# A four-layer cross-attention kernel: forty-eight projections go from plain float32 to three reduced-precision passes, and five hand-sized pieces of work move between engines

## The reference, cut to what matters

```python
# L0: cross-attention on ctx, 16 heads of 16, then an MLP (256 -> 1024 -> 256)
q = layer_norm(x) @ q_w + q_b;  k = ctx @ k_w + k_b;  v = ctx @ v_w + v_b
x = x + attention(q, k, v) @ cproj_w + cproj_b;  x = x + mlp(layer_norm(x))
# L1: queries from x, keys and values from [ctx, x] (256 keys), 16 heads of 16, then an MLP
q = x @ q_w + q_b;  k, v = split(concat([ctx, x]) @ kv_w + kv_b)
# L2: twice a cross-attention on ctx with 16 heads of 128 and one extra key and value, then an MLP
# L3: self-attention on x (w_qkv, mask), cross-attention on ctx (w_q, w_kv, mask), then an MLP
q, k, v = split(layer_norm(x) @ w_qkv + b_qkv)        # L3s
q = layer_norm(x) @ w_q + b_q;  k, v = split(ctx @ w_kv + b_kv)   # L3c
```

## Time and profile before

| | us |
|---|---|
| median of 3 runs | 1060.3 |
| lowest and highest | 1059.1 and 1060.75 |
| the profiled execution | 1061.92 |
| its span, first to last instruction | 1060.7 |
| stage A, layer 2, stage C (from the chain of waits, about) | 0 to 300, 300 to 805, 805 to 1060.7 |

### The profile page before, as it was taken

The page is one execution under the profiler, slowest core; times in us unless marked ns, Lnnn a source line. Parts: engine busy times, 40 slices in busy tenths (PEclk is TensorE's granted clock), DMA queues, the critical chain, the costliest instruction groups (busy, mean ns, idle before and its releaser), DMA issues.

```text
span 1060.7 us, 20845 instructions
## 1 busy us (share of the span) xinstructions
PE 1032.2 (97%) x8080; PEld 917.0 (86%) x8080; DVE 714.9 (67%) x1086; ACT 596.2 (56%) x1311; POOL 601.7 (57%) x627
## 2 busy tenths in 40 slices
PE   8999999999999999999999999999998999989988
PEld 7787888878888999999988999999998888778877
DVE  6987888899366565565567655665654378988751
ACT  6988788878633333223344223333226499999963
POOL 6874557465654344343287333553525689999860
PEclk9999999999999999999999999999999999999999
DMA  9200001000112222211130101110100000000000
GB/s 339 98 2 1 2 1 41 2 1 2 51 60 80 80 81 66 74 40 62 41 102 12 50 21 40 41 40 22 30 1 1 1 1 1 2 1 2 11 11 21
DMA packets 33786, 40.71 MB, mean 38 GB/s; under 512 B 2111, under 2 KB 31257, under 8 KB 32025
## 3 DMA queue, kind: packets, MB, share of 16 engines
q1 hardware_dynamic: 33689, 39.38, 11.4%
HBM read 38.32 MB, written 1.05 MB: 37 GB/s over the span
## 4 chain that ended last, share of the span: by engine, by line
PE 74%; POOL 8%; DVE 8%; ACT 5%; issue 5%; POOLq 0%; DVEq 0%; ACTq 0%
PE psum L789 14%; PE psum L683 9%; PE psum L671 8%; PE psum L803 7%; PE psum L849 7%; PE psum L709 5%; PE psum L837 5%; PE psum L817 4%; PE psum L602 4%; PE psum L699 3%; PE psum L724 2%; POOL C tile L1565 2%; PE psum L826 2%; PE psum L656 2%; ACT C tile L1364 2%
## 5 line engine op out<-in xcount | busy, mean ns | idle before, releaser
L1658 POOL TENSOR_TENSOR B tile<-B tile,B rec 128x1024 f32<-128x1024 f32 x32 | 60.8, 1899 | 204.2 <-DVE B rec L1150 204.2
L1571 POOL TENSOR_TENSOR A tile<-A tile,outer rec 128x1024 f32<-128x1024 f32 x48 | 90.7, 1897 | 74.7 <-DVE outer rec L1039 74.7
L1426 ACT ACTIVATE B own<-B max 128x8 f32<-128x8 f32 x32 | 6.7, 209 | 163.9 <-DVE B tile L1137 163.9
L1364 ACT ACTIVATE A tile<-A tile,outer min 128x128 f32<-128x128 f32 (+1 forms) x256 | 92.3, 452 | 6.1 <-DVE outer min L1032 6.0
L1282 ACT ACTIVATE B kT<-psum,B bcol 128x1024 f32<-128x1024 f32 x32 | 35.7, 1117 | 91.6 <-PE psum L789 91.6
L1364 ACT ACTIVATE C tile<-C tile,outer min 128x128 f32<-128x128 f32 x256 | 78.0, 402 | 2.1 <-DVE outer min L1032 2.1
L1178 DVE TENSOR_TENSOR x_all<-x_all,psum 128x512 f32<-128x512 f32 x64 | 42.6, 685 | 54.3 <-PE psum L849 54.3
L803 PE MATMUL psum<-B v hi,B cT hi 128*128 128x256 f32 x256 | 74.1, 289 | 0.3 <-ACT B kT L1282 0.3
L803 PE MATMUL psum<-B v hi,B cT lo 128*128 128x256 f32 x256 | 72.4, 283 | 0.0
L803 PE MATMUL psum<-B v lo,B cT hi 128*128 128x256 f32 x256 | 72.4, 283 | 0.0
L930 DVE TENSOR_SCALAR B qT<-psum,B bcol 128x1024 f32<-128x1024 f32 x32 | 41.1, 1283 | 43.3 <-PE psum L789 43.3
(11 more groups left out here) (240 smaller groups left out, 3362.4 us busy)
## 6 DMA issues: line engine op xcount, KB each, us to landing
weights<-in_weights_c SPq DMA_DIRECT2D x6, 1024.0 KB, 6.6
raw<-in_wq SPq DMA_DIRECT2D x32, 128.0 KB, 2.6
raw<-in_wk SPq DMA_DIRECT2D x32, 128.0 KB, 3.0
raw<-in_wv SPq DMA_DIRECT2D x16, 256.0 KB, 2.8
raw<-in_wo SPq DMA_DIRECT2D x16, 256.0 KB, 2.8
weights<-in_weights_a SPq DMA_DIRECT2D x1, 3072.0 KB, 21.7
weights<-in_weights_a SPq DMA_DIRECT2D x1, 2048.0 KB, 11.2
wide<-in_bias_v SPq DMA_DIRECT2D x2, 1024.0 KB, 11.5
```

What stands on the lines that cost most here:

```text
L1364: i = act.activation(of_head, of_head, ACT.Exp, bias=part.min[:, u % 4, h:h + 1], scale=-1.0)
L1571: pool.tensor_tensor(tile(u, ly.nk), tile(u, ly.nk), part.rec[:, u % 4, 0:ly.per].unsqueeze(2).to_broadcast([P, ly.per, ly.nk]), ALU.mult) ...
L1658: pool.tensor_tensor(tv, tv, m.brec[:, h, :].unsqueeze(2).to_broadcast([P, B, S]), ALU.mult).then_inc(s["normalised"].sem, s["normalised"] ...
```

## The change

- **Three passes** (`by_parts`, and `values`): keys and values of L0; queries, keys and values of L1; queries, keys and values of L3s; keys and values of L3c. The queries of L0 and of L3c stay float32. Each call has twelve fp32r matmuls in place of four float32 ones.
- **Their operands.** `ctxT_all` is gone: ACT writes the hi part of the context from PSUM at the start, DVE the lo part, and layer 2 uses the same two. `ctx_parts` goes. The input of L1 is drained by ACT (hi) and DVE (lo). That of L3s goes like that of an MLP: DVE applies scale and offset, ACT rounds, POOL subtracts.
- **Splitting their weights** (`wcut`): L0's key weights on ACT and DVE at the head of the lists; L0's value weights and the three of L1 on POOL in stage A; those of L3s on POOL in turns 5, 6 and 7 of the second attention, the two of L3c in turns 5 and 6.
- **MLP weights:** M2's four quarters are split in turns 1 to 4, L3c's four also in turns 1 to 4, behind the division of the second head, instead of in stage C.
- **The means' shares:** in stage C the shift is one DVE operation for both sequences instead of two on POOL.
- **All eight lists are written anew**, with other banks for many steps.
- The two `Bacc` constructors get `dynamic_dma_scratch_size=1024`.

```diff
@@ tensor_program
+    def by_parts(event, signal, drain, weights, src, k):
+        claim(d.take(event, k), drain, event)
+        for n in range(2):
+            for c in range(C):
+                for wp, sp in PASSES:
+                    i = pe.matmul(bank(k)[:, n * T:(n + 1) * T], weights[wp][:, c, n * P:(n + 1) * P], src[sp][:, c, :],
+                                  start=(c, wp, sp) == (0, 0, 0), stop=c == C - 1 and wp == 1)
+        i.then_inc(s[signal].sem, s[signal].mark(event))
...
-            by_features((name, "k", k, src), "k_projected", "k_drained", layers[name].wk, layers[name].sources(m, k)[src], 0, z)
+            by_parts((name, "k", k, src), "k_projected", "k_drained", m.w_parts[name, "k"], layers[name].sources(m, k)[src], z)
...
-                    i = pe.matmul(bank(z)[:, b * D:(b + 1) * D], ly.sources(m, k)[src][:, c, b * P:(b + 1) * P], ly.wv[:, c, :], start=c == 0, stop=c == C - 1)
+                    for wp, sp in PASSES:
+                        i = pe.matmul(bank(z)[:, b * D:(b + 1) * D], src[sp][:, c, b * P:(b + 1) * P], m.w_parts[name, "v"][wp][:, c, :],
+                                      start=(c, wp, sp) == (0, 0, 0), stop=c == C - 1 and wp == 1)
@@ vector_program
+            elif what == "xn" and st == "C":
+                name, of, k = a
+                dve.wait_ge(s["rstd_made"].sem, s["rstd_made"].at((name, of, k)))
+                dve.scalar_tensor_tensor(out=part.nb[k][:, :], in0=part.mv[k][:, :, 0], scalar=-1.0, in1=part.rstd[k][:, :], op0=ALU.mult, op1=ALU.mult).then_inc(
+                    s["shift_made"].sem, s["shift_made"].mark((name, of, k)))
+            elif what == "ctx":
+                k = a[0]
+                dve.wait_ge(s["ctx_hi_made"].sem, s["ctx_hi_made"].at(("ctx", k)))
+                dve.tensor_tensor(m.cT(k)[1], bank(d.bank["ctx", k]).rearrange("p (c t) -> p c t", c=C), m.cT(k)[0], ALU.subtract).then_inc(
+                    s["ctx_lo_made"].sem, s["ctx_lo_made"].mark(("ctx", k)))
+            elif what == "wcut" and tuple(a) == ("L0", "k"):
...
-            elif what == "ctx_parts":
...
@@ gpsimd_program
+    def cut_weights(name, which):
+        (hi, lo), raw, event = m.w_parts[name, which], m.w_raw[name, which], (name, which)
...
+        pool.tensor_copy(hi, raw).then_inc(s["w_hi_made"].sem, s["w_hi_made"].mark(event))
+        pool.wait_ge(s["w_hi_made"].sem, s["w_hi_made"].at(event))
+        pool.tensor_tensor(lo, raw, hi, ALU.subtract).then_inc(s["w_lo_made"].sem, s["w_lo_made"].mark(event))
...
-        if j == 2 and 2 <= turn < 5:
-            cut_up("M2", turn - 2)
+        if j == 2 and 1 <= turn < 5:
+            cut_up("M2", turn - 1)
+        if j == 2 and turn >= 5:
+            cut_weights("L3s", "qkv"[turn - 5])
...
         if turn:
             divide(j, turn, 1)
-        if last and j == 2:
-            pool.wait_ge(s["bv_drained"].sem, s["bv_drained"].at((2, NP_ - 1, 3)))
-            cut_up("M2", 3)
+        if j == 2 and 1 <= turn < 5:
+            cut_up("L3c", turn - 1)
+        if j == 2 and 5 <= turn < 7:
+            cut_weights("L3c", "kv"[turn - 5])
@@ the head of ORDER_ONE["PE"]
-    ctx 0 4, k L0 0 0 3, turn_in L0 in 0 5, ctx 1 7, q L0 0 4, k L0 1 0 5, scores 0, ctx 2 7, ctx 3 4, turn_in L0 in 1 5, scores 1, v L0 1 0 5,
+    ctx 0 0, turn_in L0 in 0 5, ctx 1 0, q L0 0 3, k L0 0 0 2, ctx 2 7, k L0 1 0 4, scores 0, k L0 2 0 7, ctx 3 5, v L0 2 0 4, scores 1,
@@ the head of ORDER_ONE["DVE"]
-    stats L0 in 0, xn L0 in 0, stats L0 in 1, q L0 0 4, stats L0 in 2, scores 0, minima 0, scores 1, even 0 0, minima 1, even 0 1, q L0 1 0,
+    stats L0 in 0, xn L0 in 0, ctx 0 0, stats L0 in 1, wcut L0 k, q L0 0 3, ctx 1 0, stats L0 in 2, stats L0 in 3, ctx 2 7, scores 0, minima 0, ctx 3 5,
```

More of the change, by code:

```diff
@@ L445 @@
+    up L1 3 2 5, up L1 3 4 7, up L1 3 6 0, turn_in L1 out 1 4, xn L1 out 2, parts 1, turn_in L1 out 0 2, parts 0, turn_in L1 out 2 3, xn L1 out 3,
+    keys_of 1, turn_in L1 out 3 7, parts 2, parts 3
 """,
     "DVE": """
-    stats L0 in 0, xn L0 in 0, stats L0 in 1, q L0 0 4, stats L0 in 2, scores 0, minima 0, scores 1, even 0 0, minima 1, even 0 1, q L0 1 0,
-    stats L0 in 3, even 1 0, scores 2, even 1 1, minima 2, scores 3, weigh 0, even 2 0, minima 3, weigh 1, even 2 1, q L0 2 2, project 1 5, project 0 0,
@@ L461 @@
-    down L1 2 1 0, stats L1 out 2, ctx_parts 1, ctx_parts 0, parts 1, down L1 3 0 0, parts 0, down L1 3 1 3, stats L1 out 3, parts 3, parts 2,
-    values_of 0, values_of 1, values_of 2, queries_of 1
+    stats L0 in 0, xn L0 in 0, ctx 0 0, stats L0 in 1, wcut L0 k, q L0 0 3, ctx 1 0, stats L0 in 2, stats L0 in 3, ctx 2 7, scores 0, minima 0, ctx 3 5,
+    scores 1, even 0 0, minima 1, even 0 1, q L0 3 3, q L0 1 0, even 1 0, scores 2, minima 2, even 1 1, even 2 0, weigh 0, scores 3, even 2 1, minima 3,
@@ L513 @@
+    up L3c 3 2 3, up L3c 3 4 0, up L3c 3 6 7
 """,
     "DVE": """
[L515 to L517 removed]
@@ L526 @@
-    turn_in L3c mlp 3 0, down L3c 2 0 7, down L3c 3 0 3, down L3c 3 1 7, down L3c 2 1 2
+    output 0, stats M2 mlp 0, output 1, xn M2 mlp 0, stats M2 mlp 1, xn M2 mlp 1, turn_in M2 mlp 0 0, output 2, stats M2 mlp 2, xn M2 mlp 2, output 3,
+    turn_in M2 mlp 1 1, stats M2 mlp 3, turn_in M2 mlp 2 5, down M2 0 0 7, down M2 0 1 3, stats L3s in 0, xn L3s in 0, xn M2 mlp 3, turn_in L3s in 0 1,
+    q L3s 0 3, scores 0, scores 1, minima 0, down M2 1 0 7, minima 1, down M2 1 1 5, stats L3s in 1, even 0 0, xn L3s in 1, down M2 2 0 1, even 0 1,
@@ L540 @@
+    stats L3c in 3, even 12 0, turn_in L3c mlp 1 4, residual L3c mlp 1, even 12 1, even 13 0, scores 14, even 13 1, scores 15, even 14 0,
+    residual L3c attn 3, even 14 1, stats L3c mlp 2, even 15 0, even 15 1, turn_in L3c mlp 2 1, stats L3c mlp 3, residual L3c mlp 2, turn_in L3c mlp 3 1,
+    residual L3c mlp 3
 """,
@@ L1583, in do @@
                 normalise(*a)
-            elif what == "xn" and xn_on(*a) == "ACT" and tuple(a[:2]) != ("L1", "mlp"):
+            elif what == "xn" and st == "A" and xn_on(*a) == "ACT" and tuple(a[:2]) != ("L1", "mlp"):
                 name, of, k = a
```

356 lines of the change are left out of this document (192 added, 164 removed).

## The result

The changed kernel takes 1065.92 us (median of 4 runs, 1065.68 to 1067.58) against 1059.92 us for the kernel before beside it: ratio 1.0059, 95% interval 1.0046 to 1.0073. It is slower by about 6 us; the forecast was 6.2 us faster. Run again with the last experiment the ratio was 1.0052 (1.0038 to 1.0066).

What follows compares the result with a forecast made beforehand. PE, 97% busy, bounds stage A and layer 2; in L3's softmax four engines are nearly full. Stage A -5.8, start +2.5, layer 2 +0.6, stage C -3.5: -6.2 us, from 1060.3 to 1054.1; range 1046 to 1061.5.

Steps and rivals of the forecast that it cites:

- A projection, stage A: Stage A's 28 projection calls, three fp32r passes instead of float32: 8 at 0.30 and 20 at 0.17 save 5.8 us.
- the middle value of 0.17 for a call alone: Saving in us for a three-pass call standing alone between float32 work, taken between 0.12 and 0.22.
- The rule of four passes: By this rule three passes cost three quarters, 1.30 us a call; 48 calls would save 20.7 us; not used.
- The start: Before stage A's first scores: keys need four parts, scores come 2.7 us later; +2.5 us taken, between 0 and 4.
- some of it returns: Part of the start's delay in stage A comes back, because PE has more projections to put behind it.
- Layer 2: Splits ahead of the second head's division in four more turns, 0.14 us each: +0.6 us; splits behind it cost nothing.
- Stage C: PE loses 4.3 us, POOL is relieved by 4.5, DVE gets 10 in 31 idle: -3.5 us, between 0 and -8.
- Rival 1: In L3, DVE's in-order list waits for POOL's rstd, delaying masks, minima and sums: slower, 1066 us; chance 0.10.
- Rival 3: New lists pack better: start absorbed, POOL's waits and low-clock stretches go; -13.2 us, 1047; chance 0.20.
- What would show it: Trace signs, among them first scores near 17 us and the stretch from L3s's first scores to last exponential 2 to 5 us shorter.
- signs of being wrong: DVE waits of several us for rstd in stage C, stage A not ending 2 us earlier, or a lone call at 1.7 us.
- DVE busier by 10: In the stretch from L3s's first scores to the last exponential, DVE's busy time grows by 10 us.

Runs made afterwards that it cites:

- the last experiment: Kernel with shifts back on POOL, where DVE also waits for each rstd and computes the shift into a tile nobody reads; 1063.26 us.
- plain_sp: Kernel with shifts back on POOL, its 48 changed calls float32 again over the hi parts alone; 1067.81 us.
- keys_first: Changed kernel with key weights' lo part made earlier, stream 0's keys projected before turning x, 20 warming transposes ahead of them; 1063.98 us.
- cut_in_c: Kernel with shifts back on POOL, the four splits of L3c's MLP weights returned to POOL's list of stage C; 1061.87 us.
- ct_late: Kernel with shifts back on POOL, the context's hi and lo parts placed after the small tiles instead of ahead of `wide`; 1057.24 us.
- op_only: Kernel with shifts back on POOL, plus a shift-like DVE operation at the 16 places into an unread tile, without waiting for rstd; 1062.79 us.
- run 6: Kernel with shifts back on POOL, the context's parts moved behind the small tiles (1057.24 us) or right behind `wide` (1059.39 us).
- start3: ct_late with the start of keys_first and DVE's subtraction for context stream 1 ahead of the drain of the queries; 1055.34 us.

## Why the prediction was wrong, step by step

- **A projection, stage A: right.** Forecast 5.8 us for 28 calls, 0.21 each; the section shrank by 5.63, and plain_sp puts the passes at 6.1. But the rows don't add up to it as I had them: in stage A's chain 16 of 18 calls take 1.41 to 1.44 us, also those that stand alone, and the float32 calls of plain_sp mostly 1.73. At 0.30 each 28 calls would be 8.4 us; where the other 2.3 go, no run shows. So the middle value of 0.17 for a call alone was partly lucky. Two rows, the second with float32 work right ahead of it:

```profile
94.49 1.42 PE psum L637 x12
121.50 1.41 PE psum L693 x12
```

- **The rule of four passes** of the Trainium skill (FP8 and Floating Point Precision, TensorE Precision Notes), as I turned it into a price, would have saved 28 x (1.73 - 1.30) = 12 us in stage A. The runs show half of that; the rows were the better guide.
- **The start: mis-sized.** Forecast +2.5, measured +5.29, of which about 1 us is the phase of the clock. I had the late lo part nearly right (11.00 to 11.68; forecast 12.2) and missed that PE idles for 3 us in front of turning x, with a granted clock of 1.2 GHz for the queries behind it in this execution, and that "some of it returns" is false: stage A gives nothing back (in the changed kernel and in keys_first the stretch behind the first scores is 248.3 and 248.5 us). The term was 2.8 us too small.
- **Layer 2: right for the splits, wrong in sum.** Forecast +0.6 for four turns; cut_in_c and ct_late put the splits at 0 to 0.3. The other 1.8 us are the moved context parts. The diff shows that move; I costed it at nothing without naming it.
- **Stage C: the step that failed.** I wrote 0.8 us a shift, "10 us in all with the drains, out of 31 idle", and let it vanish in idle time. The size was right (8.3 / 9 = 0.93 us), the cover was not: moved back to POOL, the shifts give back 6.8 us of the kernel, and op_only shows that their held time alone costs 3.6. The lists have masks, minima and sums right behind the shifts, for which ACT and PE wait. With one dip of the clock taken as 1.5 us, the section went from 270.3 to 274.1 us, +3.7 where the forecast was -3.5. The gain beside it was too large as well: with the shift on POOL (268.64, no dip) it is -1.7. The passes bring 2.5 us there, where I had 4.3, and L3s's own twelve calls only 0.6.
- **Rival 1 gave the right time (1066) by the wrong mechanism.** It had DVE wait for POOL's `rstd`, from 3.1 us of mean wait on. DVE waits 0.8 us in all, and that wait alone costs nothing. The cause is what I put beside it as the reason, the hold on the operation itself; I should have priced it as a rival of its own. That the number came out is luck. Nor did the 1.68 us fit the rule as I cited it: they are of `ve`, a TENSOR_SCALAR with one SBUF input. Rival 3 was right that the lists are better, and wrong that this would show.
- **What would show it.** Of the signs of being wrong, one fired: stage A ended 0.3 us earlier (268.19 against 268.53), not 2. DVE did not wait several us for `rstd`, and no call took 1.7 us alone (1.69 at most). "DVE busier by 10" came true (9.65 us over 841 to 1025: 149.2 to 158.8), POOL less busy too; the stretch went the other way.

## What to carry to other kernels

Before moving a small operation from POOL to DVE, look in the trace at what its form takes on DVE while POOL works, not at its free length, and choose a form that isn't held: here a reduction of the same two numbers took 0.13 us where a two-input operation took 0.8, and the difference was 3 to 4 us of the kernel. Spare time in a window's total covers nothing if the operation stands ahead of the work that the others wait for. After any change of allocations, compare the length of unchanged matmuls before blaming the new code, and give a spare tile in an experiment the same check: here 32 bytes were worth 1.6 us one way in layer 2 and 0.75 the other way in stage A. Before comparing one section of two profiles, count the dips of the clock in each.

## What the runs showed of the hardware

- Of DVE's small operations from SBUF to SBUF, the TENSOR_SCALAR and the SCALAR_TENSOR_TENSOR are held while POOL is in an operation (0.75 and 0.93 us in the mean, up to 2.30; 0.17 and 0.11 where POOL was in none); RECIPROCAL (203 ns, 206 at most, 21 of 31 inside a POOL operation), the aggregation (173 ns, 183 at most) and TENSOR_REDUCE (134 ns, 147 at most) beside the same POOL operations are not.
- In these 19 kernels an unchanged matmul of 512 columns, the key product of layer 2, takes 8 ns longer (400 against 392) where its moving and stationary operands begin 32 bytes apart, counted modulo 64: layer 2 is 1.6 to 1.9 us longer then, of 520. The products of 256 columns compared in run 6 go the other way by 1 to 2 ns; stage A is 0.7 to 0.8 us longer in all four kernels in which its region begins 32 bytes off a multiple of 64.
- In the changed kernel's start the granted clock was at 1.2 GHz until 14.17 us in one execution and until 11.82 in another, but for 3.41 us at 2.4 GHz from 4.99 on; that one fell while PE was idle for 3.28 us. In start3, with 20 warming transposes from 5.18 us on and no idle time of PE above 1.64 us in the first 30, it was at 2.4 GHz from 4.43 us and stayed.
